# Selective scan on one Trainium2 core: one unit in 24 is weighed by VectorE, and four small jobs move one or two places later

## The reference

```python
def step(h, inp):
    ul, dl, Bl, Cl = inp
    dA = jnp.exp(dl[..., None] * A)
    h = dA * h + (dl * ul)[..., None] * Bl[:, :, None, :]
    y = jnp.einsum('bkdn,bkn->bkd', h, Cl)
    return (h, y)
...
dts = jnp.einsum('bkrl,kdr->bkdl', dts, dt_proj_w)
delta = jax.nn.softplus(dts + dt_proj_b[None, :, :, None])
...
y = (y1 + y2 + y3 + y4)
```

## Time and profile before

| | before |
|---|---|
| median of 3 runs | 11102.96 us (11083.56 to 11105.95) |
| profiled execution: its own time, its span | 11114.08 us, 11112.4 us |
| PE, PEld busy share of the span | 88%, 59% |
| DVE busy | 85% |
| ACT busy | 78% |
| POOL busy | 81% |
| mean granted PE clock | 0.954 of 2.4 GHz |

### The profile page before, as it was taken

How to read it: one execution, slowest core, us unless ns; L and a number is a source line. 1 busy time by engine, 2 the same in 40 slices (tenths; PEclk the granted TensorE clock), 3 DMA queues, 4 the chain that set the end, 5 groups by cost and what they waited for, 6 DMA issues and landing times. The chain is left out here.

```text
span 11112.4 us, 345302 instructions
## 1 busy us (share of the span) xinstructions
PE 9796.2 (88%) x142892; PEld 6546.6 (59%) x142892; DVE 9404.3 (85%) x5727; ACT 8689.8 (78%) x15618; POOL 9035.1 (81%) x3978
## 2 busy tenths in 40 slices
PE   8978888888888888888888888888888889799999
PEld 5645555555555555555555555555555555588888
DVE  7869999998999999989999998999999999555554
ACT  3468888888888888888888888888888888345453
POOL 1169999999999999999999999999999999534330
PEclk9989999999999999999999999999999999899999
DMA  3356666666666666666666666666666666322220
GB/s 103 108 153 160 167 174 171 161 167 170 174 161 167 177 167 162 168 173 167 159 167 175 166 161 166 175 170 162 172 177 164 159 171 163 84 75 64 70 70 13
DMA packets 547249, 1647.95 MB, mean 148 GB/s; under 512 B 148562, under 2 KB 149362, under 8 KB 542872
## 3 DMA queue, kind: packets, MB, share of 16 engines
q1 hardware_dynamic: 484248, 1416.10, 50.0%
q10 hardware_dynamic: 61440, 209.76, 6.1%
...
## 5 line engine op out<-in xcount | busy, mean ns | idle before, releaser
L1004 POOL TENSOR_TENSOR HC<-H,crep 128x1024 f32<-128x1024 f32 x3072 | 7203.9, 2383 | 358.0 <-PE psum L714 277.7
L779 DVE TENSOR_TENSOR_SCAN H<-E,car,psum 128x1024 f32<-128x1024 f32 x2304 | 5271.4, 2333 | 344.8 <-PE psum L691 111.2
L880 ACT ACTIVATE E<-dlr,am 128x1024 f32<-128x1024 f32 x3072 | 3497.2, 1145 | 917.2 <-DVE H L779 868.6
L714 PE MATMUL psum<-HC,sely 128*32 128x512 f32 x12288 | 2307.0, 635 | 83.4 <-POOL HC L1004 65.2
L779 DVE TENSOR_TENSOR_SCAN H<-E,psum 128x1024 f32<-128x1024 f32 x768 | 1713.5, 2273 | 173.4 <-PE psum L691 78.1
L691 PE MATMUL psum<-diagp,dluT 128*32 128x128 f32 x49152 | 1630.3, 276 | 256.0 <-DVE H L779 240.8
L691 PE MATMUL psum<-diag,dluT 128*32 128x128 f32 x49152 | 1692.7, 280 | 145.7 <-issue 121.1
L691 PEld LDWEIGHTS psum<-diagp,dluT 128*32 128x32 f32 x49152 | 1387.0, 111 | 681.0 <-DVE H L779 488.9
L691 PEld LDWEIGHTS psum<-diag,dluT 128*32 128x32 f32 x49152 | 1448.2, 112 | 496.0 <-issue 377.3
L862 ACT ACTIVATE sdl<-dluT,blt 128x192 f32<-128x192 f32 x4096 | 1507.5, 444 | 0.0
L680 PE MATMUL psum<-idn,sdl 128*128 128x128 f32 x6144 | 953.2, 305 | 566.2 <-DVE H L779 566.2
...
## 6 DMA issues: line engine op xcount, KB each, us to landing
dlr<-scr_dl SPq DMA_DIRECT2D x3072, 128.0 KB, 4.2
dur<-scr_dlu SPq DMA_DIRECT2D x3072, 128.0 KB, 3.3
crep<-scr_bc SPq DMA_DIRECT2D x512, 256.0 KB, 6.4
crep<-scr_bc SPq DMA_DIRECT2D x1024, 128.0 KB, 3.0
scr_dlu<-dlu SPq DMA_DIRECT2D x256, 384.0 KB, 3.1
scr_yk<-yt ACTq DMA_DIRECT2D x256, 384.0 KB, 3.0
scr_dl<-dlt ACTq DMA_DIRECT2D x128, 384.0 KB, 4.4
scr_dl<-yt ACTq DMA_DIRECT2D x128, 384.0 KB, 4.2
```

Source lines behind the costliest of these rows:

```text
L714: r = e.matmul(yps[32 * j:32 * j + 32, cols], sely[:], HC[:, (3 * i + j) % NHC, cols], start=g == 0 and k != 0 and not second(m), stop=g = ...
L779: e.tensor_tensor_scan(H[:, un % NH, ::step], decay[:, ::step], drive[:, ::step], init, ALU.mult, ALU.add).then_inc(scan_done)
L880: e.activation(E[:, un % NE, :], dlr[:, slot(m, j), :], ACT.Exp, scale=am[:, ae:ae + 1]).then_inc(exp_done)
L1004: e.tensor_tensor(HC[:, un % NHC, :], H[:, un % NH, :], crep[:, g, :], ALU.mult).then_inc(hc_done)
```

## The change

DVE weighs one unit of each pair itself: place 21 (n odd, x = 9). Its scan writes back into the PSUM tile of its drive (`out = drive`), and a `tensor_tensor` straight after it multiplies that tile by C into HC. POOL leaves that unit out. The unit takes no slot of H; its PSUM tile is free only after this multiplication, and after ACT has copied its last column (`own_carry`). POOL's two diagonals come after its weighing of places 19 and 20, which before came after places 18 and 20.

Apart from that, `split` is done by DVE after the scan of place 7 and no longer of place 6; the two `dt` jobs stand at x = 7 and 9 (before 6 and 8), the two softplus at x = 9 and 11 (8 and 10), POOL's first `delta` at x = 10 (8), and the two stores of delta one place later. `bt` stays at x = 10.

```diff
     DIAG_AT = 14
+    OWN = tuple(n % 2 == 1 and x == 9 for n in range(2) for x in range(12))
     PARTS = 2
-    POOL_AT = (7, 9)
+    POOL_AT = (8, 9)
...
+    def own(un):
+        return OWN[un % 24]
+
+    def owns(un):
+        return un // 24 * sum(OWN) + sum(OWN[:un % 24])
+
+    def others(un):
+        return un - owns(un)
...
             if x == 4 and c < NCHUNK:
                 jobs += [("x", c)]
-            if x == 6 and c < NCHUNK:
+            if x == 7 and c < NCHUNK:
                 jobs += [("dt", 2 * c)]
-            if x == 8 and c < NCHUNK:
+            if x == 9 and c < NCHUNK:
                 jobs += [("dt", 2 * c + 1)]
             if x == 10 and c < NCHUNK:
                 jobs += [("bt", c)]
...
     def bank_free(e, *job):
         i = place_of[job] - NP
-        if i >= 0:
-            e.wait_ge(released[ring[i][0]], ring[i][1] + 1)
+        if i < 0:
+            return
+        name, n = ring[i]
+        if name == "unit" and own(n):
+            e.wait_ge(own_hc_done, owns(n + 1))
+            if has_carry(n):
+                e.wait_ge(own_carried, own_carries(n))
+        else:
+            e.wait_ge(released[name], n + 1)
...
-            if un >= NH:
-                e.wait_ge(hc_done, un - NH + 1)
-            if has_carry(un - NH):
-                e.wait_ge(carried, carries(un - NH))
-            if ci:
+            out, at = H[:, others(un) % NH, :], others(un) - NH
+            if own(un):
+                out = drive
+            elif at >= 0:
+                e.wait_ge(hc_done, at + 1)
+                if has_carry(in_H[at]):
+                    e.wait_ge(carried, carries(in_H[at]))
+            if ci and own(un):
+                e.wait_ge(own_carried, own_carries(un - 24))
+            elif ci:
                 e.wait_ge(carried, carries(un - 24))
             step = 1 if k < 2 else -1
-            e.tensor_tensor_scan(H[:, un % NH, ::step], decay[:, ::step], drive[:, ::step], init,
+            e.tensor_tensor_scan(out[:, ::step], decay[:, ::step], drive[:, ::step], init,
                                  ALU.mult, ALU.add).then_inc(scan_done)
+
+        def weigh(un):
+            b, k, ci, half, m, g, j = place(un)
+            e.wait_ge(scan_done, un + 1)
+            e.wait_ge(crep_in[load_of(g)], 64 * (m // 2 + 1))
+            if un >= NHC:
+                e.wait_ge(y_summed, (un - NHC) // 3 + 1)
+            e.tensor_tensor(HC[:, un % NHC, :], bank("unit", un), crep[:, g, :], ALU.mult).then_inc(own_hc_done)
...
             scan(un)
-            if c < NCHUNK and n % 2 == 0 and x == 6:
+            if own(un):
+                weigh(un)
+            if c < NCHUNK and n % 2 == 0 and x == 7:
                 split(c)
...
+        def own_carry(un):
+            last = TC - 1 if place(un)[1] < 2 else 0
+            e.wait_ge(own_hc_done, owns(un + 1))
+            e.copy(car[:, cell(un):cell(un) + 1], bank("unit", un)[:, last:last + 1]).then_inc(own_carried)
...
-                if x == 9:
+                if x == 10:
                     out_dl(2 * c)
-                if x == 11:
-                    out_dl(2 * c + 1)
+            if n < NSTEP and n % 2 and c < NCHUNK and x == 0:
+                out_dl(2 * c + 1)
...
+            if has_carry(un - 1) and own(un - 1):
+                own_carry(un - 1)
...
-                if x == 8 and c < NCHUNK:
+                if x == 9 and c < NCHUNK:
                     delta(2 * c)
-                if x == 10 and c < NCHUNK:
+                if x == 11 and c < NCHUNK:
                     delta(2 * c + 1)
-                if x == 11 and c < NCHUNK:
                     turn_b(c)
...
-            if un:
+            if un and not own(un - 1):
                 weigh(un - 1)
...
-                if x == 8 and n + 2 < NSTEP:
+                if x == 10 and n + 2 < NSTEP:
                     delta(n + 2)
```

More of the change, by code:

```diff
@@ L1 @@
 from contextlib import ExitStack
+import itertools
 import numpy as np
@@ L407, in scan_phase @@
     hc_done = sem("hc_done")
+    own_hc_done = sem("own_hc_done")
     carried = sem("carried")
+    own_carried = sem("own_carried")
     y_summed = sem("y_summed")
@@ L441, in last_of, with ends @@
                    and kind(un) in want.get("kinds", (DIRECT, DIAGONAL, SCALED)))
+    def own(un):
[4 more added lines that the diff above has]
+        return un - owns(un)
+    in_H = [un for un in range(NUNIT) if not own(un)]
+    def ends(t, a, b):
+        return t[:, a:b + 1:b - a] if b > a else t[:, a:b - 1 if b else None:b - a]
     def slot(m, j):
@@ L467, in has_carry, with own_carries @@
         return 0 <= un < NUNIT and place(un)[2] < NCH - 1
+    pairs_to = list(itertools.accumulate(int(has_carry(un) and not (own(un) and own(un + 1))) for un in range(0, NUNIT, 2)))
+    own_to = list(itertools.accumulate(int(has_carry(un) and own(un)) for un in range(NUNIT)))
     def carries(un):
-        m, x = divmod(un, 12)
-        line, rest = divmod(m, 2 * NCH)
-        return 6 * (line * (2 * NCH - 2) + min(rest, 2 * NCH - 2)) + (x // 2 + 1 if rest < 2 * NCH - 2 else 0)
+        return pairs_to[un // 2]
+    def own_carries(un):
+        return own_to[un]
     def second(m):
@@ L564, in in_crep @@
             if c:
-                e.wait_ge(hc_done, max(last_of(2 * c - 1, g=g) for g in groups) + 1)
+                last = max(last_of(2 * c - 1, g=g) for g in groups)
+                e.wait_ge(hc_done, others(last + 1))
+                e.wait_ge(own_hc_done, owns(last + 1))
             g0, n = groups[0], len(groups)
@@ L711, in sum_y @@
             if sub == 0:
-                e.wait_ge(hc_done, 3 * (i + 1))
+                e.wait_ge(hc_done, others(3 * (i + 1)))
+                if owns(3 * (i + 1)) > owns(3 * i):
+                    e.wait_ge(own_hc_done, owns(3 * (i + 1)))
             for j in range(NJ):
@@ L883, in carry @@
             last = TC - 1 if place(un)[1] < 2 else 0
-            c0, c1 = cell(un - 1), cell(un)
-            cells = car[:, c0:c1 + 1:c1 - c0] if c1 > c0 else car[:, c0:c1 - 1 if c1 else None:c1 - c0]
             e.wait_ge(scan_done, un + 1)
-            e.copy(cells, H[:, (un - 1) % NH:un % NH + 1, last]).then_inc(carried)
+            a, z = cell(un - 1), cell(un)
+            if own(un):
+                e.copy(car[:, a:a + 1], H[:, others(un - 1) % NH, last:last + 1]).then_inc(carried)
+            else:
+                e.copy(ends(car, a, z), ends(H[:, :, last], others(un - 1) % NH, others(un) % NH)).then_inc(carried)
+        def own_carry(un):
+            last = TC - 1 if place(un)[1] < 2 else 0
+            e.wait_ge(own_hc_done, owns(un + 1))
+            e.copy(car[:, cell(un):cell(un) + 1], bank("unit", un)[:, last:last + 1]).then_inc(own_carried)
         def copy_y(m):
@@ L1003, in weigh @@
                 e.wait_ge(y_summed, (un - NHC) // 3 + 1)
-            e.tensor_tensor(HC[:, un % NHC, :], H[:, un % NH, :], crep[:, g, :], ALU.mult).then_inc(hc_done)
+            e.tensor_tensor(HC[:, un % NHC, :], H[:, others(un) % NH, :], crep[:, g, :], ALU.mult).then_inc(hc_done)
         delta(0)
```

## The result

The change made the kernel slower: 11309.56 us median of 4 runs (11292.85 to 11327.19) against 11104.45 us, a ratio of 1.0187 with a 95% interval of 1.0163 to 1.021. That is 205 us, or 1.6 us a pair. The forecast was slower by about 79 us, 0.62 us a pair.

The account below looks back on a forecast made before the run. DVE's work and waits, not POOL alone, were taken to set the pair: -1.95 - 1.78 + 1.25 + 2.3 + 0.8 = +0.62 us, 127 times +79 us on 11103, so 11180 us; range 10990 to 11320.

Parts of the forecast that it names:

- POOL leaves out place 21: Scan of place 1 on DVE no longer waits for POOL's weighing of place 21: -1.95 us a pair.
- what follows on PE and ACT: Later fill of place 24 on PE and ACT's wait at own_carry are covered: 0 us.
- The split: DVE's split one unit later no longer waits for ACT's copy of sx: -1.78 us a pair.
- The weighing on DVE: DVE's added multiplication takes +1.25 us a pair; its scan writing into PSUM adds 0.
- The wait in front of it: DVE's weighing of place 21 waits for PE's sum of places 15 to 17: +2.3 us a pair, ends 1.6 and 3.1.
- The dt jobs and the softplus: Moving them later frees place 11 and loads place 13: +0.8 us a pair, ends 0 and 1.5.
- The +1.2 for place 13: Scan of place 13 waits longer, as its fill on PE must wait for the second softplus: +1.2 us.
- -0.4 for place 11: Fill of place 11 no longer stands behind the second dt job, so most of its wait goes: -0.4 us.
- Faster: Rival: softplus hidden and PE fast at place 22, -1.28 us a pair, 10940 us; chance 0.30.
- POOL as the bound: Stronger form of the faster rival: POOL alone bounds, 2.385 us off each pair, 10800 us; chance 0.03.
- Much slower: Rival: PE's idle stretches drop its clock at places 13 and 21, +3.4 us a pair, 11530 us; chance 0.07.
- the likeliest case: The prediction's own case, chance 0.48: 11130 to 11290 us, with stall 1.9 to 2.9 and place 13 term 0.5 to 1.2.

Follow-up runs that it names:

- e1: Changed kernel with the moved small jobs back at their places (POOL's diagonals stay moved), DVE still weighing place 21: 11231.08 us, 1.0112 of the kernel before.
- e2: Changed kernel with the moved jobs alone, POOL weighing all units and DVE none: 11134.06 us, 1.003 of the kernel before.
- e3: Changed kernel with DVE weighing place 22 and not 21, ACT's carry copying the other unit: 11109.09 us, 1.0003 of the kernel before.
- e8: Changed kernel (place 21) with job bt and ACT's copy of it one place later: 11151.34 us, 1.0042 of the kernel before.
- e9: Changed kernel with DVE weighing place 22, and bt and ACT's copy of it one place later: 10933.79 us, 0.9848 of the kernel before.
- e10: Changed kernel with DVE weighing place 22, bt two places later and ACT's copy at x = 1: 10895.7 us, 0.9814 of the kernel before.
- e11: Changed kernel with bt one place later and nothing weighed by DVE: 10958.36 us, 0.9873 of the kernel before.
- e12: Changed kernel with bt two places later and nothing weighed by DVE: 10921.14 us, 0.9837 of the kernel before.

## Why the prediction was right in its sign and wrong in its size

Idle time of DVE by place, us a pair:

| idle before | before | e1 | e2 | change | e3 | e8 | e9 | e10 |
|---|---|---|---|---|---|---|---|---|
| scan of place 1 | 1.83 | 0.03 | 1.72 | 0.02 | 0.22 | 0.03 | 0.19 | 0.21 |
| split | 1.78 | 1.60 | 0.03 | 0.03 | 0.03 | 0.03 | 0.03 | 0.03 |
| multiplication of 7 | 0.03 | 0.03 | 0.28 | 0.17 | 0.19 | 0.17 | 0.21 | 0.19 |
| multiplication of 11 | 0.33 | 0.34 | 0.10 | 0.14 | 0.03 | 0.08 | 0.04 | 0.02 |
| scan of 13 | 0.59 | 0.30 | 1.95 | 1.90 | 2.33 | 0.00 | 0.00 | 0.00 |
| scans of 12 and 14 | 0.35 | 0.31 | 0.51 | 0.60 | 0.55 | 1.35 | 1.36 | 0.42 |
| scan of 18 | 0.62 | 0.64 | 0.78 | 0.83 | 0.68 | 0.85 | 0.78 | 1.12 |
| DVE's weighing | | 2.35 | | 2.52 | 0.47 | 2.44 | 0.49 | 0.70 |
| everything | 6.22 | 6.06 | 6.20 | 6.75 | 5.09 | 5.47 | 3.67 | 3.37 |
| length of a pair | 68.90 | 69.76 | 68.98 | 70.54 | 68.86 | 69.12 | 67.34 | 67.13 |

**POOL leaves out place 21: right.** The scan of place 1 no longer waits. The gain was 1.81 us and not 1.95: the prediction's rows show 1.97 us in one pair, and the mean of the pairs is 1.83. The scans of places 0 and 1 don't wait for the tile of place 21 either, so the 0 for what follows on PE and ACT was right. That this is all DVE gets from POOL is right as well: its saved 2.4 us a pair turned into idle time, 235.9 to 643.8 us in the window. POOL's work a pair is now 4593.7 + 341.8 + 228.2 + 223.7 us over 85 pairs, 63.4 us, against the 63.3 worked out.

**The split: right**, from 1.78 us a pair to 0.03. Of this about 0.1 us came back ahead of the multiplication of place 7, which waits now and then for its fill.

**The weighing on DVE: right.** 1225 ns against 1.25 us. The scan into PSUM takes 2334 ns, as the one into H: the 0 was right.

**The wait in front of it: right in mechanism and, partly by luck, nearly in size.** 2.53 us a pair against 2.3. e3 shows that it is a cost of its own: one place later, 2.05 us of it and 200 us of time go. e1 adds that it comes without the moved jobs too (2.35). The lower end of 1.6 us was right. The upper end was not: the long waits are 4.1 us on the mean and not 3.1. In the pair with 4.20 us PE is slow in both halves of the sum, where in rows 6 it was fast again in the second. They come in a third of the pairs (30 of 85) and not half. The two errors nearly cancel in the middle that I took.

**The dt jobs and the softplus: the step that failed, by its size.** I forecast +0.8 us a pair, and it was +1.7. The chain is as forecast: bt behind scan 11, the fill behind the softplus, 1.4 us forecast for the scan of place 13 and 1.56 measured in a pair at full clock. The +1.2 for place 13 came out as 1.90 - 0.59 = +1.3, but partly by luck. With the fill at full clock the wait rose from 0.21 to 1.16 us on the mean, by 0.95. The other 0.36 is the clock: the fill was slow in 39 of 84 pairs, up from 20 of 86, and I had priced that only in a rival with a chance of 0.07. The mis-sized parts are two others. I took -0.4 for place 11, as if all idle time before multiplications, 0.46 us, stood there; 0.33 did, and it fell by 0.19. And I put nothing, without a reason, at the places around it: the multiplication of place 7 and the scans of places 12, 14 and 18 wait 0.14, 0.07, 0.18 and 0.21 us a pair longer, 0.6 together. e2 has nearly the same without the weighing, so they belong to the moved jobs.

The 0.9 of this term, the 0.2 of the stall and the 0.14 of place 1 make 1.25 us a pair. Against them stand about 0.2 us of waits at places 2 and 23 that went and 0.1 us because rows of scans back to back overlap. The pair came out 70.55 - 68.87 - 0.62 = 1.1 us over the forecast, so the sum closes to about 0.1.

e8 confirms that this term is the ring's and can be taken out: 158 us with one job a place later. The edit removes both parts of it, the standing still and the slow fills, so the 0.95 and 0.36 above are counted from pairs and not shown by a run that changes one alone. Why the clock falls in some pairs at this place and not in others, no run shows.

**The rivals.** Faster (0.30 + 0.03): the place 13 term was not hidden, and POOL as the bound is refuted by e2, e11 and e12. Much slower (0.07): it happened in part, and at place 13 alone, from 20 slow fills in 86 pairs to 39 in 84. Before the new weighing PE's slow pairs were as frequent as before the change: the fill of place 22 is slow in 37% of the pairs in both, and the mean granted clock is 0.954 in both profiled executions. The range ended at 11320, which holds the time, but the likeliest case's own range of 11130 to 11290 does not.

**What stays open.** Why the fill of place 13 is slow in fewer pairs with the weighing alone (8 of 85), and in more with place 22 (55 of 86). Why place 18 waits longer with the moved jobs. And bt one place later without any other moved job was not tried.
